# Causal masks and their unit matrix in fp32r, and the third group's first score tile ahead of the values' products

## The reference

```python
scores = jnp.einsum('bhqd,bhkd->bhqk', q, k) * scale
causal = jnp.triu(jnp.full((t, t), -jnp.inf, dtype=scores.dtype), k=1)
attn = jax.nn.softmax(scores + causal, axis=-1)
```

## Time and profile before

| | |
|---|---|
| median of 3 runs | 3649.94 us (3648.4 to 3652.1) |
| the profiled execution's own time | 3651.66 us |
| its span, first to last instruction | 3649.9 us |
| mean granted TensorE clock | 0.989 of full speed |
| PE busy | 3549.6 us (97%) |
| PE weight loads busy | 2676.6 us (73%) |
| DVE busy | 3088.9 us (85%) |
| ACT busy | 2422.8 us (66%) |
| POOL busy | 1827.4 us (50%) |

### The profile page before, as it was taken

How to read it: one execution, slowest core, us unless ns; L and a number is a source line. 1 busy time by engine, 2 the same in 40 slices (tenths; PEclk the granted TensorE clock), 3 DMA queues, 4 the chain that set the end, 5 groups by cost and what they waited for, 6 DMA issues and landing times.

```text
span 3649.9 us, 88155 instructions
## 1 busy us (share of the span) xinstructions
PE 3549.6 (97%) x30735; PEld 2676.6 (73%) x30990; DVE 3088.9 (85%) x7415; ACT 2422.8 (66%) x5698; POOL 1827.4 (50%) x2967
## 2 busy tenths in 40 slices
PE   7999999999999999999999999987999999999998
PEld 6888888888888888888888888875555555555554
DVE  6888888888888888888888888876989989989987
ACT  4777777777777777777777777774554555554554
POOL 5776677666776667766777667763001001001000
PEclk9999999999999999999999999988999999999999
DMA  3444444444444444444444444433222222212211
GB/s 102 119 120 106 117 115 120 114 111 116 117 120 112 114 113 120 116 111 114 117 120 115 113 117 115 120 88 81 65 65 78 71 58 81 75 55 80 73 45 54
DMA packets 298324, 361.76 MB, mean 99 GB/s; under 512 B 28192, under 2 KB 264992, under 8 KB 297888
## 3 DMA queue, kind: packets, MB, share of 16 engines
q1 hardware_dynamic: 297888, 356.11, 37.2%
HBM read 131.80 MB, written 53.26 MB: 51 GB/s over the span
## 4 chain that ended last, share of the span: by engine, by line
PE 86%; DVE 7%; DMA 2%; issue 2%; SPq 1%; ACT 0%; POOL 0%; DVEq 0%; another core or an unknown queue 0%; POOLq 0%
PE ps L1077 14%; PE ps L1411 11%; PE ps L1165 8%; PE ps L1126 7%; PE ps L1113 7%; PE ps L1420 6%; PE ps L1196 5%; PE ps L1150 5%; PE ps L1215 4%; PE ps L1205 3%; PE ps L1173 3%; PE ps L1435 2%; PE ps L1427 2%; PE ps L1154 2%; PE ps L1198 2%
## 5 line engine op out<-in xcount | busy, mean ns | idle before, releaser
L1077 PE MATMUL ps<-xb,w_tok 128*128 128x196 f32 x3072 | 686.3, 348 | 7.5 <-DMA clsT<-in_clsT 7.3
L1411 PE MATMUL ps<-X,cn_w 128*128 128x394 f32 x1536 | 584.9, 510 | 7.7 <-DVE X L1015 7.7
L886 DVE TENSOR_REDUCE mx<-ps 69x2 f32<-69x396 f32 x1024 | 518.0, 553 | 14.2 <-PE ps L1205 1.3
L592 ACT ACTIVATE p<-ps 128x394 f32<-128x394 f32 x1024 | 454.8, 499 | 74.6 <-PE ps L1126 65.3
L1077 PEld LDWEIGHTS ps<-xb,w_tok 128*128 128x128 f32 x3072 | 491.7, 192 | 8.0 <-DMA clsT<-in_clsT 7.3
L880 DVE TENSOR_REDUCE mx<-ps 128x4 f32<-128x512 f32 x512 | 337.6, 680 | 181.1 <-remote 180.2
L543 POOL TENSOR_SCALAR ve<-mv 128x4 f32<-128x4 f32 x64 | 20.2, 316 | 911.7 <-DVE mv L898 911.7
L1411 PEld LDWEIGHTS ps<-X,cn_w 128*128 128x128 f32 x1536 | 273.6, 189 | 258.0 <-issue 94.9
L537 POOL TENSOR_TENSOR h<-h,att 128x256 f32<-128x256 f32 (+1 forms) x256 | 186.9, 751 | 431.9 <-DVE att L875 431.9
L1126 PE MATMUL ps<-qZ,kT 128*128 128x396 f32 (+1 forms) x2048 | 382.5, 320 | 12.9 <-DMA qZ<-mx_scratch 11.0
L610 ACT ACTIVATE sq<-ps 128x256 f32<-128x256 f32 (+1 forms) x512 | 196.2, 383 | 247.1 <-PE ps L1113 247.1
(11 more groups left out here) (139 smaller groups left out, 8076.5 us busy)
## 6 DMA issues: line engine op xcount, KB each, us to landing
qZ<-qT SPq DMA_DIRECT2D x256, 396.0 KB, 5.2
xb<-in_x SPq DMA_DIRECT2D x128, 588.0 KB, 7.2
kZ<-kT SPq DMA_DIRECT2D x512, 128.0 KB, 2.6
h_scratch<-h SPq DMA_DIRECT2D x128, 128.0 KB
hl<-h_scratch SPq DMA_DIRECT2D x64, 256.0 KB
hk<-h_scratch SPq DMA_DIRECT2D x64, 256.0 KB
out<-hk SPq DMA_DIRECT2D x64, 256.0 KB
h_scratch<-h SPq DMA_DIRECT2D x128, 69.0 KB
```

Source lines behind the costliest of these rows:

```text
L592: s.activation(p0[:, i, 2 * jj:2 * jj + 2, :], ps[:, (b0, b1)[jj], 0:2 * TE].rearrange("p (a b) -> p a b", b=TE)[:, :, 0:T], ACT.Exp).then ...
L886: v.tensor_reduce(mx[:T1, 1, 4 * i + c:4 * i + 4:2], ps[:T1, SBANK[3 * i + 1 + c], 0:2 * TE].rearrange("p (a b) -> p a b", b=TE), AX.X, AL ...
L1077: mm = t_.matmul(ps[:, W[ft], 0:NP], w_tok[:, k, ft * P:ft * P + P], xb[:, par, k, :], start=k == 0, stop=k == KT - 1)
L1411: mm = t_.matmul(ps[:, 2 * c + mt, 0:N2], cn_w1[:, f, mt * P:mt * P + P], X[:, c, state(cyc), f, :], start=f == 0, stop=f == FT - 1)
```

## The change

The two masks become fp32r (a 4-byte form) and are multiplied with `ident_r`, the fp32r unit matrix that is there already for the transposes of queries and keys; `ident_b` and its cast on DVE go. `mask0` and `mask1` are cleared and filled on POOL as before, now at 4 bytes an element.

In PE's step, `scores_first(m, 2)` with its wait for `kZ_loaded[1]` moves from behind both `pv` to ahead of them, right behind `hn_transpose`. For that, group 2's first tile takes bank 1, which the first tile of group 1 has left, and its wait is for `s_max` 2 in place of 4; banks 0 and 1 are exchanged in the tables of the other uses. The later wait for `kZ_loaded[1]` stays in place, ahead of `scores_halves`.

```diff
-        ident_b = sb("ident_b", [P, P], BF16)
-        mask0 = sb("mask0", [P, 4, P], BF16)
-        mask1 = sb("mask1", [P, 2, E1], BF16)
+        mask0 = sb("mask0", [P, 4, P], F32R)
+        mask1 = sb("mask1", [P, 2, E1], F32R)
...
-        SBANK = (6, 7, 0, 1, 2, 3, 0, 1, 2, 3, 0, 5)
-        MAX_OF = (4, 2, 5, 6, 7)
+        SBANK = (6, 7, 0, 1, 2, 3, 1, 0, 2, 3, 1, 5)
+        MAX_OF = (2, 4, 5, 6, 7)
-        KB, QB = (3, 4, 0, 5), (1, 2, 3, 4)
+        KB, QB = (3, 4, 1, 5), (0, 2, 3, 4)
-        MB, CB = (7, 0), (1, 2)
+        MB, CB = (7, 1), (0, 2)
...
-            v.tensor_copy(ident_b[:], ident[:]).then_inc(s_cv, 1)
...
-                t_.matmul(ps[:, b, :], ident_b[:], mask0[:].rearrange("p a b -> p (a b)"),
+                t_.matmul(ps[:, b, :], ident_r[:], mask0[:].rearrange("p a b -> p (a b)"),
...
-                    t_.matmul(tail, ident_b[:T1, :T1], mask1[:T1], start=False, stop=True).then_inc(s_done, 1)
+                    t_.matmul(tail, ident_r[:T1, :T1], mask1[:T1], start=False, stop=True).then_inc(s_done, 1)
...
+                if there(m):
+                    pe.wait_ge(kZ_loaded[1], n * 32)
+                    scores_first(m, 2)
                 if there(o):
                     if there(m):
                         pe.wait_ge(s_max, n * 12 - 11)
...
                 if there(m):
                     pe.wait_ge(kZ_loaded[1], n * 32)
-                    scores_first(m, 2)
                     scores_halves(m, 1 - r % 2, 2)
```

More of the change, by code:

```diff
@@ L311, in build @@
         ]
-        N_CV = 11
+        N_CV = 10
         N_CP = 16
@@ L452, in _ @@
             g.memset(ident[:], 0.0).then_inc(s_cp, 1)
-            g.memset(mask0[:], 0.0).then_inc(s_cp, 1)
-            g.memset(mask1[:], 0.0).then_inc(s_cp, 1)
+            g.memset(mask0[:].bitcast(F32), 0.0).then_inc(s_cp, 1)
+            g.memset(mask1[:].bitcast(F32), 0.0).then_inc(s_cp, 1)
             g.memset(sign[:], 1.0).then_inc(s_cp, 1)
@@ L463, in _ @@
                             pattern=[[-1, P]], channel_multiplier=1).then_inc(s_cp, 1)
-            g.affine_select(out=mask0[:], in_=mask0[:], compare_op=ALU.is_ge, fill=NEG, base=0,
+            g.affine_select(out=mask0[:], in_=mask0[:].bitcast(F32), compare_op=ALU.is_ge, fill=NEG, base=0,
                             pattern=[[0, 4], [-1, P]], channel_multiplier=1).then_inc(s_cp, 1)
-            g.affine_select(out=mask1[:], in_=mask1[:], compare_op=ALU.is_ge, fill=NEG, base=0,
+            g.affine_select(out=mask1[:], in_=mask1[:].bitcast(F32), compare_op=ALU.is_ge, fill=NEG, base=0,
                             pattern=[[0, 2], [-1, E1]], channel_multiplier=1).then_inc(s_cp, 1)
@@ L779, in _ @@
             v.tensor_scalar(wq_row[:], wq_row[:], float(HD) ** -0.5, None, ALU.mult).then_inc(s_cv, 1)
-            dve.wait_ge(s_cv, 10)
+            dve.wait_ge(s_cv, 9)
             v.tensor_tensor(wk_row[:], wk_row[:], wq_row[:], ALU.mult).then_inc(s_cv, 1)
```

## The result

The changed kernel takes 3639.51 us (median of 15 runs, 3635.86 to 3645.51) against 3649.96 us (15 runs, 3644.18 to 3653.8): a ratio of 0.9972 [0.9964, 0.998], 10.4 us less or 0.28%. The forecast was 3647.9, 2.0 us less and within 0.2%, in a range of 3636 to 3661. The time lies in the range, near its low end and near rival A's 3637; the forecast's own case did not come.

What follows compares the result with a forecast made beforehand. The prediction took PE's own instruction stream in the attention stage as the bound. The order's -19.0 us and the masks' +17.0 us gave -2.0 us, from 3649.94 to 3647.9 us, with a range of 3636 to 3661 us.

Steps and rivals of the forecast that it cites:

- rival A: Attention steps: the moved tile pays and the fp32r masks cost little, 3637 us; chance 0.28.
- the forecast's own case: Whole kernel: the two edits nearly cancel, 3647.9 us, within 0.2% of before; chance 0.52.
- What bounds the kernel: Attention stage: PE's own instruction stream sets the step, 18.94 us; other waits matter only if PE arrives too early.
- The order: Moved scores tile in PE's step: one change of array division less, 0.15 us a step, 19.0 us in all.
- The new change from strips to halves: L1215 directly behind `pv`: taken to cost 0.13 us, bounds nothing and 0.28 us.
- The masks on PE: Twelve mask matmuls a step in fp32r: 12 + 40 + 81 = 133 ns a step more, 17.0 us over 128.
- the first load of each series: Weight load ahead of each series of 140-column masks: 27 ns more, three times a step, 81 ns.
- The 128-column load: fp32r unit-matrix load for the 512-column masks: stays hidden, counted as nothing; 384 ns a step if in sight.
- The sum: Whole kernel: -19.0 + 17.0 = -2.0 us, giving 3647.9 us.
- The new wait on group 1's maximum: Moved tile's wait for `s_max` 2: should not hold PE, margin 0.15 to 0.2 us.
- Rivals B, C and D: Unit-matrix load in sight, 3697 us (0.09); group 1's maximum late, 3661 (0.04); strips-to-halves costing both changes, 3667 (0.07).
- The waits for the keys: PE's waits for padded keys at first scores, 6.3 us: nothing more expected, 2 us at most over the run.

Runs made afterwards that it cites:

- after: The changed kernel itself, moved tile and fp32r masks together, against the kernel before: 3639.51 us against 3649.96, ratio 0.9972.
- order_only: Against the changed kernel, masks and their unit matrix back in bfloat16, moved tile and exchanged banks kept: 3630.46 us.
- tile_masks_r: Against the changed kernel, the 140-column masks back in bfloat16, only the 512-column masks left in fp32r: 3634.14 us.

## Why the prediction was right in its range and wrong in its sum

- What bounds the kernel: right for 18.8 us of a step, and the error is in the rest. "What counts in this stage is how long PE's own instruction stream is" took the stream as unbroken. It had two waits of about 0.1 us in every step, for ACT's first copy of the projection and for DVE's last maximum. The first is shown by the pair of runs with one more mask, the second by the constant distance from DVE's end to PE's load.
- The order, 0.15 us a step and 19.0 us: right, mechanism and size. 0.147 us and 18.9 us. The new change from strips to halves costs what the one from the whole to halves does (0.34 for the L1215 behind it), as I had chosen; the chance that it is free was not needed.
- The masks on PE, 133 ns a step: right in size, 0.14 by the chain. Its parts: L1198 12 ns, in fact nothing; the first load of each series 27 ns, in fact 28 by the starts of the loads (0.031 to 0.059 us between the first two of a series, in all three series); the rest of it 5 ns a mask and more at the end of a series. The 27 ns came out by luck in the working: 0.03 us of load in sight, grown in proportion to the load (112 to 141 ns), gives 8 ns and not 27, which is nearly the whole difference of the loads. The whole difference is what was measured. With 8 ns the sum would have been -9.3 us, nearer to the result for a wrong reason. The 128-column load stayed hidden, as the form of two L1196 in a row had shown.
- **The step that failed**: "Together the masks add 12 + 40 + 81 = 133 ns a step, 17.0 us over 128." On PE's own pieces they do, but they add only 0.103 us to the step and 10.5 us to the time: 0.035 us and 0.02 us go into the two waits. By the step alone it would be 13 us; whether the last 3 us come back through fewer waits for the keys or are noise is open. I had looked for cover of the order's parts and not of the masks', for which the question was the same: what is late next behind this instruction. The rows to read were those of the second projection against the first, 0.98 and 0.88 us in the chain before, for the same columns.
- The sum, -2.0 us, should have been some -8.5 by the two parts; the changed kernel measured -10.4 us in the first series of runs and -8.5 in the second, and the intervals overlap. Rival A had the right sign and nearly the size, for a reason that did not hold: it had the first masks' loads better hidden.
- The new wait on group 1's maximum: right, it held in no step. In the step shown DVE's two maxima start at 1215.26 and end 1.29 us later at 1216.55, the load of the moved tile stands at 1216.76, 0.21 us behind, as worked out; over the whole trace the load is never less than 0.116 us behind. The wait for `kZ_loaded[1]` at the moved tile has no row either. Rivals B, C and D did not come.
- The waits for the keys: I took them as unchanged. They were 3 us shorter in the changed kernel's traces, though no run shows that this reached the time, and moving the DMAs was worth 6 us.

## What to carry to other kernels

When an engine seems to run without a gap, compare the same piece of work in two places of the step: where it takes longer, there may be a wait that no row names, and what is added ahead of it there is free until the wait is used up. Whether it is one, the code's wait and a constant distance to the other engine's end tell. Adding one harmless instruction at each of two places tells in one pair of runs which stretch is covered. Two edits that reach the chip together should be run apart: here one gained 18.9 us and the other took 10.5 of it back.

## What the runs showed of the hardware

- Going from strips of 32 columns straight to 64-row halves costs PE what going from the whole array to halves does (0.34 us up to the projection in either place, in `after` and `order_only`); by the estimate from the earlier trace rows that is 0.13 us. Strips to the whole array costs 0.15 (0.147 by the step of `order_only`). Here the order alone saved one of the three changes in a row.
- A mask in fp32r over 512 columns takes as long as in bfloat16 (0.23 to 0.24 us; a step of 18.814 us with either, in `tile_masks_r` and `order_only`), although its load has 189 ns in place of 96. By the loads' starts the bfloat16 load was not issued until the matmul ahead of it had gone by (0.235 us from the load before it, against 0.12 for the fp32r one), which reads as if the short load was in sight and the long one is not; why it is issued later is not shown. Over 140 columns it is the other way round, 0.41 us for four against 0.36.

```profile
L1196 PEld LDWEIGHTS ps<-mask,ident_r 128*128 128x128 f32 x512 | 97.0, 189 | 0.0
L1203 PEld LDWEIGHTS ps<-mask,ident_r 69*69 69x69 f32 x1024 | 93.6, 139 | 107.1 <-issue 89.8
```
